# Edge lists of a four-layer graph network loaded in the setup block by ScalarE's queue, 16 source gathers placed there, semaphores cleared by TensorE

## The reference

```
h = relu(layernorm(x)); x = x + gat(h, edges)            # attention, softmax over the edges of a dst
h = relu(layernorm(x)); x = x + gatv2(h, edges, attr16)  # attention, batch norm, gelu
h = relu(layernorm(x)); x = x + edge_attention(h, edges, attr18)   # softmax over the edges of a src
h = relu(layernorm(x)); x = x + gru_rounds(h, edge_weight, edges, edge_type)  # 2 message rounds
```

## Time and profile before

| | us |
|---|---|
| median of 3 runs (6470.49 to 6482.01) | 6478.54 |
| the profiled execution, its own time | 6449.81 |
| its span in the trace | 6447.9 |
| busy: DVE, POOL, PE, ACT | 4686.6, 4514.4, 4092.2, 3159.7 |
| setup, first instruction to the last DVE operation | 0.3 to 32.6 |
| q, first to last operation | 33.8 to 42.4 |
| prep, first to last POOL instruction | 43.7 to 609.1 |
| l0 begins | 616.1 |

### The profile page before, as it was taken

One profiled execution on the slowest core, in us unless ns is written; L12 is line 12 of the kernel. 1 busy time (PEld: TensorE's weight loads), 2 busy tenths in 40 slices (PEclk: granted clock), 3 DMA queues, 4 the chain that ended last, 5 costly groups with the idle time before them and its releaser, 6 DMA issues. The chain is left out here.

```text
span 6447.9 us, 85793 instructions
## 1 busy us (share of the span) xinstructions
PE 4092.2 (63%) x15111; PEld 2125.7 (33%) x15111; DVE 4686.6 (73%) x9073; ACT 3159.7 (49%) x5462; POOL 4514.4 (70%) x4877
## 2 busy tenths in 40 slices
PE   0101555555569999799987777774899777777600
PEld 0000211111134444466643333332444344444300
DVE  5884988888869999667645555555899666766667
ACT  0111444444457777678766666665666433333200
POOL 4777888888866664556537888886888577777743
PEclk9999555555589999899978888887999887788755
DMA  2442322222256666899963444443344333333388
GB/s 87 137 147 63 80 77 73 77 74 76 70 138 174 173 173 162 153 186 194 194 126 112 113 114 114 117 113 91 86 95 96 62 71 71 70 69 69 65 317 318
DMA packets 949964, 773.07 MB, mean 120 GB/s; under 512 B 661199, under 2 KB 727708, under 8 KB 945875
## 3 DMA queue, kind: packets, MB, share of 16 engines
q1 hardware_dynamic: 819859, 614.72, 32.6%
q0 software_dynamic: 125504, 131.83, 13.8%
q10 hardware_dynamic: 4512, 25.60, 1.0%
HBM read 472.43 MB, written 310.28 MB: 121 GB/s over the span
## 5 line engine op out<-in xcount | busy, mean ns | idle before, releaser
L205 ACT ACT_TABLE_LOAD x511 | 655.6, 1283 | 137.3 <-PEq L66 128.4
L954 POOL DMA_INDIRECT x<-l_out,l_snum x392 | 475.9, 1214 | 106.5 <-issue 90.1
L918 POOL DMA_INDIRECT l_rows<-x,l_num x392 | 443.4, 1131 | 148.2 <-issue 93.4
L954 POOL DMA_INDIRECT m<-l2s_out,l2s_snum x392 | 439.6, 1122 | 148.7 <-issue 105.7
L1159 POOL DMA_INDIRECT pre_src_rows<-in_x,all_idx_src x392 | 396.7, 1012 | 164.5 <-issue 130.2
L918 POOL DMA_INDIRECT l_rows<-in_x,l_num x392 | 430.0, 1097 | 105.7 <-issue 90.5
L918 POOL DMA_INDIRECT l2s_rows<-vc_rows,l2s_num x392 | 416.3, 1062 | 106.3 <-issue 95.5
L918 POOL DMA_INDIRECT l_rows<-eo,l_num x392 | 386.5, 986 | 148.5 <-issue 97.1
L954 POOL DMA_INDIRECT xg<-l3b_out,l3b_snum x392 | 394.9, 1007 | 114.2 <-issue 88.5
L918 POOL DMA_INDIRECT l3a_rows<-m,l3a_num x392 | 391.7, 999 | 106.3 <-issue 89.6
L918 POOL DMA_INDIRECT l3b_rows<-g_rows,l3b_num x392 | 387.2, 988 | 106.2 <-issue 92.1
(11 more groups left out here) (407 smaller groups left out, 13600.9 us busy)
## 6 DMA issues: line engine op xcount, KB each, us to landing
l_far<-far_d SPq DMA_DIRECT2D x196, 256.0 KB, 3.7
xg<-l2s_bg_row SPq DMA_DIRECT2D x97, 512.0 KB, 3.8
dl_xin<-xg SPq DMA_DIRECT2D x31, 1600.0 KB
l2s_bg_x<-x SPq DMA_DIRECT2D x97, 260.0 KB, 3.0
x<-ts_row SPq DMA_DIRECT2D x31, 812.5 KB, 4.5
l_keep<-keep_d SPq DMA_DIRECT2D x196, 128.0 KB, 6.0
xs<-l_xT SPq DMA_DIRECT2D x98, 256.0 KB
hs<-l_hT SPq DMA_DIRECT2D x98, 256.0 KB, 3.2
```

The source lines that it names most:

```text
L205: act.add_instruction(mybir.InstLoadActFuncSet(name=nc.get_next_instruction_name(), ins=[], outs=[], act_func_set_id=which))
L918: pool.indirect_dma_start(self.buf[k.q][:, j, at:at + w], None, table, bass.IndirectOffsetOnAxis(ap=self.num[k.q][:, m, j:j + 1], axis=0)) ...
L954: pool.indirect_dma_start(self.table, bass.IndirectOffsetOnAxis(ap=self.num[k.q][:, j:j + 1], axis=0), self.out[k.q][:, j, 0:self.cols], N ...
```

## The change

The source list and the others get a scope `prep` that is opened ahead of setup, and what fills and loads them moves into the setup block: POOL fills the source tile ahead of the 13 memsets and the other tiles behind them; ACT issues the 31 loads, the five of `src` first on a semaphore of their own; DVE and PE turn the source column ahead of everything else they do there; POOL then issues the first 16 (`EARLY`) of the 392 source gathers at the end of its part of setup. The block of the sort (scope `sort` now) begins without fills and loads, turns the other columns and issues the remaining 376 gathers. Apart from that, no scope ends with a clearing block any more: the semaphores of the stages left are cleared by PE at the head of its stream in the next stage, and given back at the next exit; one clearing block stays at the very end.

```diff
 class Scope:
     def __exit__(self, *a):
-        if self.used and a[0] is None:
-            with self.nc.Block() as block:
-                @block.gpsimd
-                def _(pool):
-                    for s in self.used:
-                        pool.sem_clear(s)
+        if a[0] is None:
+            for stack in Scope.cleared:
+                stack.close()
+            Scope.cleared.clear()
+            Scope.left.extend(self.used)
+            Scope.kept_back.append(self.sem_stack)
+            if self is Scope.whole:
+                with self.nc.Block() as block:
+                    @block.gpsimd
+                    def _(pool):
+                        Scope.clear_left(pool)
...
+    def clear_left(eng):
+        for s in Scope.left:
+            eng.sem_clear(s)
+        Scope.cleared.extend(Scope.kept_back)
+        Scope.left.clear()
+        Scope.kept_back.clear()
...
+def lists_beside_setup(nc, c, s, src, dst, weight, etype, x):
...
+    def fill_src(pool):
+        pool.memset(s.isrc[:], PAD_NODE).then_inc(s.filled, 1)
+    def fill(pool):
+        pool.memset(s.icur[:], PAD_NODE).then_inc(s.filled, 1)
...
+    def gathers(pool):
+        hold(pool, c.src_known, 1)
+        for j in range(c.EARLY):
+            pool.indirect_dma_start(c.src_rows[:, j, :], None, x, bass.IndirectOffsetOnAxis(ap=c.idx_src[:, j:j + 1], axis=0)
+                                    ).then_inc(c.src_gathered, 16)
+    def load(act):
+        act.wait_ge(s.filled, 1)
+        for b, rows in enumerate(blocks):
+            act.dma_start(s.isrc[0:rows, b, :], src[b * P * P:b * P * P + rows * P].rearrange("(r f) -> r f", f=P)).then_inc(s.src_loaded, 16)
...
+        act.wait_ge(s.filled, 9)
...
+    def columns(dve):
+        step = Chain(dve, s.head_step)
+        dve.wait_ge(s.src_loaded, 16 * (NBLK + 1))
+        step(dve.tensor_copy(s.key[0][:], s.isrc[:].rearrange("p b f -> p (b f)")))
+        step(dve.tensor_scalar(s.key[1][:], s.key[0][:], float(c.N) - 0.5, None, ALU.is_lt))
+        step(dve.tensor_tensor(s.pay[1][:], s.key[0][:], s.key[1][:], ALU.mult))
+        dve.sem_inc(s.head_pay, 1)
+        dve.wait_ge(s.head_turned, 1)
+        step(dve.tensor_copy(c.idx_src[:], s.ptk[:, 0:c.NT]))
+        dve.sem_inc(c.src_known, 1)
+    def turn(pe):
+        pe.wait_ge(s.head_pay, 1)
+        for b in range(NBLK):
+            ins = pe.transpose(s.ptk[:, b * P:(b + 1) * P], s.pay[1][:, b * P:(b + 1) * P], c.ident[:])
+        ins.then_inc(s.head_turned, 1)
...
@@ prep_lists, block of the sort
-                for lst, out in ((icur, c.idx_dst), (isrc, c.idx_src)):
+                for lst, out in ((icur, c.idx_dst),):
...
-                dve.sem_inc(c.src_known, 1)
...
             @block.tensor
             def _(pe):
+                Scope.clear_left(pe)
...
@@ setup
             @block.gpsimd
             def _(pool):
+                fill_src(pool)
                 pool.memset(c.ident[:], 0.0).then_inc(filled, 1)
...
                 pool.memset(c.zero_rows[:], 0.0).then_inc(filled, 1)
+                fill(pool)
                 pool.wait_ge(filled, 13)
...
+                gathers(pool)
+            @block.scalar
+            def _(act):
+                load(act)
...
                 step = Chain(dve, step_s)
+                columns(dve)
                 dve.wait_ge(filled, 17)
...
+                Scope.clear_left(pe)
                 pe.wait_ge(filled, 17)
+                turn(pe)
                 pe.wait_ge(loaded, 16 * loads[0])
...
@@ tables_start
-        hold(pool, c.src_known, 1)
-        for t in range(c.NT):
+        for t in range(c.EARLY, c.NT):
```

More of the change, by code:

```diff
@@ L54, in __init__ @@
     def __init__(self, nc, name):
-        self.nc, self.name, self.stack, self.used = nc, name, ExitStack(), []
+        self.nc, self.name, self.stack, self.sem_stack, self.used = nc, name, ExitStack(), ExitStack(), []
     whole = None
+    left, kept_back, cleared = [], [], []
     def __enter__(self):
@@ L63, in __exit__ @@
     def __exit__(self, *a):
-        if self.used and a[0] is None:
-            with self.nc.Block() as block:
-                @block.gpsimd
-                def _(pool):
-                    for s in self.used:
-                        pool.sem_clear(s)
-        return self.stack.__exit__(*a)
+        if a[0] is None:
[9 more added lines that the diff above has]
+                        Scope.clear_left(pool)
+                for stack in Scope.cleared:
+                    stack.close()
+                Scope.cleared.clear()
+        return self.stack.__exit__(*a)
+    @staticmethod
+    def clear_left(eng):
[4 more added lines that the diff above has]
+        Scope.kept_back.clear()
     def sb(self, name, shape, dt=F32):
@@ L216, in prep_lists @@
+def prep_lists(nc, c, s, src, dst, weight, etype, dram, beside):
     E = src.shape[0]
@@ L218, in prep_lists @@
     beside_act, beside_sync, beside_pool, row_piece = beside
-    full, rest = E // P, E % P
-    blocks = [min(P, full - b * P) for b in range(NBLK)]
-    with Scope(nc, "prep") as s:
+    with Scope(nc, "sort") as r:
         ident = c.ident
[L223 to L242, removed]
+        key, pay, icur, iprev, inext, isrc, ityp, nrm, idx_i, sgn_i = (
+            s.key, s.pay, s.icur, s.iprev, s.inext, s.isrc, s.ityp, s.nrm, s.idx_i, s.sgn_i)
+        filled, loaded, loads, ptk, ptp = s.filled, s.loaded, [s.loads], s.ptk, s.ptp
+        swap = r.sb("swap", [P, NBLK * P // 2], I32)
+        cur = r.sb("cur", [P, NBLK, P])
+        oth = r.sb("oth", [P, NBLK, P])
+        start = r.sb("start", [P, NBLK, P])
+        flag = r.sb("flag", [P, NBLK, P])
+        sgn = r.sb("sgn", [P, 1])
+        keys_ready, pay_copied = (r.sem(n) for n in ("keys_ready", "pay_copied"))
+        dve_step, turned, stored, last_pay, to_store = (r.sem(n) for n in ("dve_step", "turned", "stored", "last_pay", "to_store"))
+        keys_stored, keys_back = r.sem("keys_stored"), r.sem("keys_back")
         levels = [(k, j) for k in range(1, 17) for j in range(k - 1, -1, -1)]
@@ L250, in _ @@
             def _(pool):
[L251 to L258, removed]
@@ L259, in _ @@
-                pool.iota(sgn_i[:], pattern=[[0, 1]], base=0, channel_multiplier=1).then_inc(filled, 1)
-                pool.wait_ge(filled, 8)
-                pool.memset(iprev[0:1, 0, 0:1], -1).then_inc(filled, 1)
                 beside_pool(pool)
-            loads = []
             @block.sync
             def _(sp):
[L269 to L286, removed]
@@ L433, in flip @@
                     return ins
-                for _ in range(4 + c.NREL):
+                for _ in range(3 + c.NREL):
                     n += 1
@@ L451, in _, with setup_tiles @@
                     flip(ptk, pay[1]).then_inc(turned, 1)
-def setup(nc, c, w):
+def setup_tiles(c):
     sc = c.scope
@@ L480, in setup @@
     c.ones_row = sc.sb("ones_row", [1, P])
+    c.quiet = [sc.sb(f"quiet{k}", [P, D]) for k in range(2)]
+def setup(nc, c, w, lists):
+    fill_src, fill, gathers, load, columns, turn = lists
     scale = float(8) ** -0.5
@@ L2040, in quiet_states @@
 def quiet_states(nc, c):
-    c.quiet = [c.scope.sb(f"quiet{k}", [P, D]) for k in range(2)]
     with Scope(nc, "q") as s:
@@ L2437, in nodes_last, with _ @@
         with nc.Block() as block:
+            @block.tensor
+            def _(pe):
+                Scope.clear_left(pe)
             @block.sync
@@ L2517, in gnn @@
         c.eps, c.one = sc.sb("eps", [P, 1]), sc.sb("one", [P, 1])
-        setup(nc, c, a)
-        quiet_states(nc, c)
+        c.EARLY = 16
+        setup_tiles(c)
         with Scope(nc, "pre") as pre:
@@ L2522, in gnn @@
           c.src_known, c.src_gathered = pre.sem("src_known"), pre.swdge_sem("src_gathered")
-          with Scope(nc, "ts") as c.start:
-            beside = tables_start(nc, c, a["x"], a["dst"], x1)
-            prep_lists(nc, c, a["src"], a["dst"], a["edge_weight"], a["edge_type_3"], dram, beside)
+          with Scope(nc, "prep") as prep:
+            lists = lists_beside_setup(nc, c, prep, a["src"], a["dst"], a["edge_weight"], a["edge_type_3"], a["x"])
+            setup(nc, c, a, lists)
+            quiet_states(nc, c)
+            with Scope(nc, "ts") as c.start:
+              beside = tables_start(nc, c, a["x"], a["dst"], x1)
+              prep_lists(nc, c, prep, a["src"], a["dst"], a["edge_weight"], a["edge_type_3"], dram, beside)
           conv_gat(nc, c, a["x"], dram, x1, e1, m2)
```

43 lines of the change are left out of this document (41 added, 2 removed).

## The result

The kernel after takes 6403.73 us (median of four runs, 6393.12 to 6411.61) where before takes 6478.15 on the same chip: ratio 0.9882, 95% interval 0.9869 to 0.9894, 74.4 us less. The prediction said 6401. The profiled execution of after took 6403.0, with a span of 6401.3; that of before is 47 longer, not 74. The gap between 47 and 74 is a question of its own, taken up first among the experiments.

What follows compares the result with a forecast made beforehand. The prediction took no engine to bound the whole kernel, DVE to bound setup and POOL prep. Its terms -56.6, -2.1 and -18.8 sum to -77.5, set against the median of 6478.54: 6401 us, range 6384 to 6422.

Steps and rivals of the forecast that it cites:

- The moved lists: In prep, gathers start at 45.8 instead of 82.12 us and the last ends at 552.5 instead of 609.10: -56.6.
- Setup changes its bound from DVE to POOL: At the end of setup, POOL's gathers decide instead of DVE, so q starts at 35.8 us, 2.0 later.
- The 4.4 us behind POOL's last gather: Time after prep's last gather that is no clearing; assumed to follow setup's last gather too.
- The bound of -3.6: At the end of setup: the forecast's error, -3.6 us, if the 4.4 us behind the last gather don't follow there.
- The joints: Between stages behind l0, dropped clearing blocks save 0.0635 us a clear and 0.4 a block end: -18.8.
- PE's clears at nothing: At stage heads, a stage's first gather hides PE's clears, at 0.0635 us each; uncovered they cost up to 18.8.
- one of my own signs of a misjudged step: In l2, PE's first product later than 4.6 us after the stage's start would mean the clears were misjudged.
- Queueing loads: In setup, ACT's and SP's loads go one after the other: q 12.1 us later, 6413 in all; chance 0.12.
- Clears that were no loss: At the joints, 287 clears (18.2 us) and eleven block ends (4.4) are not won: 6424; chance 0.08.
- DVE as prep's bound: In prep, gathers at 1.23 us throughout let DVE decide at 542.7: 6387 in all; chance 0.07.
- Clears that make it slower: At stage heads, PE's clears at 0.44 us each eat the gain and 37 us of cover; chance 0.04.
- The sum: Whole kernel: -56.6 for prep, -2.1 for the joint behind it, -18.8 for later joints: -77.5 us.

Runs made afterwards that it cites:

- e4: The kernel after with none of the source gathers issued in setup (EARLY 0 instead of 16): 6397.97 us, ratio 0.9909 to before.
- e6: The kernel after with 32 source gathers issued in setup instead of 16: 6390.25 us, ratio 0.9895 to before.
- e9: The kernel after with the 31 list loads on SP's queue instead of ACT's: 6385.16 us, ratio 0.9883 to before.
- e2: The kernel before with only the clearing blocks dropped and PE's clears added, lists unmoved: 6439.00 us, ratio 0.9968 to before.
- e10: Second run of the kernel after without a block for q, whose instructions stand in the sort's block: 6360.94 us, ratio 0.9856 to before.
- e7: The kernel after with each of PE's clears done four times, the very last block unchanged: 6431.12 us, ratio 0.9956 to before.
- e5: The kernel after, unchanged, run and profiled again: 81.0 us below before, ratio 0.9882.
- e8: First run of the kernel after without a block for q, whose instructions stand in the sort's block: 6366.01 us, ratio 0.9861 to before.

## Why the prediction was right, and which steps were not

*The moved lists.* Forecast: first gather 10.5, 376 gathers from 45.8 to 552.5, DVE done at 542.7, l0 at 557.4. Measured in the two profiles of after: 10.89, from 45.65 to 549.11 and from 45.94 to 553.51, 543.89 and 544.51, l0 at 553.44 and 557.84. The pace over all 376 was 1.339 and 1.350 us, which alone makes the 4 us between them. That POOL goes on bounding prep held; e4 and e6 move the bound to either side of it.

*Setup's bound was wrong.* "Setup changes its bound from DVE to POOL", q 2.0 later: q came 0.94 and 1.23 later and behind DVE. Two terms were off. The 4.4 us behind POOL's last gather were taken over from prep; with its block end it is 3.04 in setup (e6), so POOL would have let q start at 33.9. And DVE ended at 34.23, not at 33.1: SP 0.3 later, the landing 3.06 instead of 2.56, DVE's work 8.10 instead of 7.76. These had been taken from a setup without gathers, and e4, without them, comes out near the forecast: SP done at 22.93, 2.55, 7.76, DVE done at 33.24. With gathers beside it DVE ends between 33.81 and 34.53 in the eight profiles that have both. The bound of -3.6 "without the 4.4 in setup" was a slip as well: by the prediction's own 33.5 instead of 35.8 it is -2.3.

*The joints.* Forecast -18.8 behind l0; the table's six joints from l1 to dl give 2.87 + 4.29 + 3.41 + 2.84 + 2.49 + 2.38 = 18.3. The model of 0.0635 a clear and 0.4 a block end stands (0.49 to 0.51 are left at q, prep and l2, where nothing else is waited for). The joint to l3b is not down to a block end, because SP waits 1.6 us at the end of l3a until the last stored rows have landed (L2211).

*PE's clears at nothing.* The conclusion held, its working did not. The price is 0.12, not 0.0635, so q pays 0.77 and not 0.4, and 63 clears run past the 4.58 that I took for l2's cover. This was one of my own signs of a misjudged step (7.62 instead of 4.6). What saved it is that the cover is longer than I read: the product that the stage waits for is the one on the first gathered rows, 13.57 into l2 in after (2550.90 in the rows above) and 13.21 in before:

```profile
2613.22 1.09 PE L1784 MATMUL l_p_oT<-all_ident,l_rows 128*128 128x128 f32 x4 [7.30 <-DMA l_rows<-eo,l_num]
```

I had taken PE's first instruction for PE's first needed one. The nothing that it put into the sum was thus right by a cover it had not read, which is luck.

*The rivals.* Queueing loads: 0.8 and not 12.1 (e9), and only 0.2 of it without the gathers (e4). Clears that were no loss: their going gave 20.9 (e2). DVE as prep's bound: not in after, nearly in e10, and in e6. Clears that make it slower, from 0.44 each on: e7 puts 0.48 on each semaphore and is still 29.5 faster than before, since the stages cover far more than 37 us.

*The sum.* -77.5 forecast, -74.4 and -81.0 measured. That the difference was set against the median and not against the profiled execution mattered: between the two profiles only 47 us are to be seen, and l2's length makes up most of what is missing.

## What to carry to other kernels

Price a move on the engine that ends the stage, from its first needed instruction to its last, breaks included: here the gain was POOL starting at 10.9 instead of 82 and, in e10, not pausing. Bookkeeping between stages cost its full length here as long as it had a block of its own; on an engine whose first needed work waits for a gather it was free up to about that point, and which point that is has to be read from the first operation on gathered rows. Before a stage's length in one profile is put down to a change, look at that stage in a second profile of the same kernel.

## What was not expected of the hardware

A clear costs 0.120 us on PE (252 in 30.23) and 0.064 on POOL (63 in 4.05). What follows POOL's last gather up to the next stage isn't one number: 3.04 at the end of setup (e6), 4.33 to 4.59 at the end of prep with 16 gathers in setup (after, e5, e8 and e10 among them), 5.00 with none there (e2, e4); what it consists of stays open. Two queues of small loads cost SP's path 0.2 at most, but 0.7 to 1.1 with gathers beside them. And l2, with its DMA engines 0.93 to 0.95 busy, took from 720 to 754 us in thirteen profiles with the same 3141 products on PE, as the granted clock went from 0.94 to 0.89; in the stretch shown it fell behind PE's short waits for loads.
